# A DLRM tower on one core: the slots' products in two halves, id products for two tables only, and one engine for the slots known ahead

## What is computed

```python
e = jnp.stack([tbl_0[ids[:, 0]], ..., tbl_25[ids[:, 25]]], axis=1)
combined = jnp.concatenate((dense_features[:, None, :], e), axis=1)
interactions = jnp.einsum('bfd,bgd->bfg', combined, combined)
z = jnp.concatenate((dense_features, interactions[:, iu, ju]), axis=1)   # iu, ju: upper triangle
h = jnp.concatenate([z, r_dense_features], axis=1)
h = jnp.maximum(h @ W_top1 + b_top1, 0.0)      # 607 x 512
h = jnp.maximum(h @ W_top2 + b_top2, 0.0)      # 512 x 256
y = h @ W_top3                                 # 256 x 1
```

## Time and profile before

| | us |
|---|---|
| median of 3 runs | 106.65 (106.25 to 109.59) |
| the profiled execution | 106.54 |
| its span in the profile | 104.70 |
| outside the span | 1.84 |
| PE busy | 95.0 (91%) |
| DVE busy | 65.8 (63%) |
| ACT busy | 47.7 (46%) |
| POOL busy | 63.7 (61%) |

### The profile page before, as it was taken

The page is one execution under the profiler, slowest core; times in us unless marked ns, Lnnn a source line. Parts: engine busy times, 40 slices in busy tenths (PEclk is TensorE's granted clock), DMA queues, the critical chain, the costliest instruction groups (busy, mean ns, idle before and its releaser), DMA issues.

```text
span 104.7 us, 3425 instructions
## 1 busy us (share of the span) xinstructions
PE 95.0 (91%) x1510; PEld 81.2 (78%) x1510; DVE 65.8 (63%) x112; ACT 47.7 (46%) x83; POOL 63.7 (61%) x66
## 2 busy tenths in 40 slices
PE   5969899999999999999999589998999879994992
PEld 5846587888888888888877389986999769993990
DVE  5259999999999999999630294205741084506121
ACT  3286799998508608902300165301834039121230
POOL 2777777787787777777777377775777760000000
PEclk9999999999999999999999999999999999999999
DMA  1999999999922211211212110111111210000000
GB/s 32 205 365 422 394 386 419 416 386 409 376 96 50 53 50 47 53 44 34 56 50 66 47 49 27 50 50 50 53 50 50 50 50 25 0 0 0 0 0 1
DMA packets 3957, 12.99 MB, mean 124 GB/s; under 512 B 1447, under 2 KB 1453, under 8 KB 3310
## 3 DMA queue, kind: packets, MB, share of 16 engines
q1 hardware_dynamic: 1874, 8.95, 22.6%
q0 software_dynamic: 1920, 3.94, 13.1%
q10 hardware_dynamic: 156, 0.02, 0.1%
HBM read 12.90 MB, written 0.00 MB: 123 GB/s over the span
## 4 chain that ended last, share of the span: by engine, by line
PE 76%; DVE 12%; DMA 4%; issue 3%; ACT 2%; ACTq 1%; DVEq 0%
PE prod L361 18%; PE bank L361 16%; PE bank L404 13%; PE prod L450 11%; PE prod L477 7%; DVE inter_s L566 4%; DMA col_sb<-in_columns 4%; PE bank L370 4%; DVE mask L502 3%; DVE low L517 2%; PE bank L317 2%; PE prod L459 2%; PE bank L486 2%; PE bank L321 2%; ACT pairs_s L678 1%
## 5 line engine op out<-in xcount | busy, mean ns | idle before, releaser
L309 POOL DMA_INDIRECT emb<-in_tbl,ids_sb x60 | 63.0, 1051 | 22.0 <-issue 16.2
L502 DVE TENSOR_SCALAR mask<-ids_h,col_sb 128x1024 fp32r<-128x1024 int16 (+1 forms) x49 | 31.0, 694 | 1.9 <-ACT ids_h L639 1.6
L566 DVE STREAM_TRANSPOSE inter_s<-prod 128x288 f32<-128x288 f32 (+1 forms) x8 | 4.6, 612 | 17.9 <-PE prod L450 17.9
L450 PE MATMUL prod<-xT 128*27 128x27 f32 x1024 | 12.9, 194 | 1.9 <-issue 0.8
L361 PE MATMUL prod<-mask,high 128*128 128x512 f32 x42 | 14.0, 396 | 0.0
L361 PE MATMUL prod<-mask,low 128*128 128x512 f32 x42 | 13.8, 390 | 0.0
L450 PEld LDWEIGHTS prod<-xT 128*27 128x27 f32 x1024 | 11.1, 103 | 3.5 <-issue 3.1
L678 ACT COPY pairs_s<-inter_s 128x117 f32<-128x117 f32 x8 | 2.3, 294 | 21.5 <-DVE inter_s L566 18.9
L511 DVE TENSOR_TENSOR low<-table,high 128x1024 fp32r<-128x1024 f32 (+1 forms) x9 | 11.4, 1301 | 0.2 <-ACT high L611 0.2
L404 PE MATMUL bank<-pairs,w_sb 117*128 117x128 f32 x96 | 11.4, 275 | 0.0
L361 PE MATMUL bank<-mask,high 128*128 128x512 f32 x36 | 11.3, 395 | 0.0
(11 more groups left out here) (56 smaller groups left out, 103.9 us busy)
## 6 DMA issues: line engine op xcount, KB each, us to landing
table<-in_resident SPq DMA_DIRECT2D x3, 1024.0 KB, 8.2
w_sb<-in_weights SPq DMA_DIRECT2D x1, 1792.0 KB, 12.9
table<-in_resident SPq DMA_DIRECT2D x1, 1280.0 KB, 12.8
table<-in_resident SPq DMA_DIRECT2D x4, 256.0 KB, 4.6
emb<-in_tbl,ids_sb POOLq DMA_INDIRECT x60, 2.8
ids_h<-in_other_ids SPq DMA_DIRECT2D x1, 640.0 KB, 11.9
table<-in_resident SPq DMA_DIRECT2D x1, 640.0 KB, 8.4
known<-in_dense_t SPq DMA_DIRECT2D x1, 256.0 KB, 11.9
```

The source lines that it names most:

```text
L309: nc.gpsimd.indirect_dma_start(out=rows(t, c), out_offset=None, in_=gathered[c], in_offset=bass.IndirectOffsetOnAxis(ap=ids_sb[:, i:i + 1] ...
L450: mm = nc.tensor.matmul(prod[SLOT_PITCH * q:SLOT_PITCH * q + SLOTS, i, 0:SLOTS], x, x, start=True, stop=True)
L502: nc.vector.tensor_scalar(made(step)[:, 0:n, :], ids_h[:, 2 * b:2 * b + n, :], col_sb[:, row:row + 1], None, ALU.is_equal).then_inc(s_mask, 1)
L566: nc.vector.transpose(blocks[:, rows, 0:MATMULS], prod[:, :, rows].rearrange("p j g -> p g j")).then_inc(s_blk, 1)
```

## The change

- Only two tables' ids are spread by TensorE (`SPREAD` 2); the ids of pair 1 come by a broadcasting DMA behind table pair 1 (`pair_ids`, 256 KB), and those of the other seven tables by one behind pair 2 (`other_ids`, 896 KB). The id products contract over 2 partitions instead of 128.
- The columns are part of `ids_sb`, and their own DMA is gone.
- `WARM_UP` goes from 4 to 6, `WARM_KEEP` from 2 to 10 products of two instructions each.
- ACT makes one mask in each of pairs 1 to 4, instead of two in pair 1 and one in pair 2. DVE makes one mask between the two lower parts of a pair. `w1_sum` moves behind all masks.
- The slots' products are split in two halves, with the turns of groups 0 and 1 of the next tile between them; group 3 is turned with group 2, ahead of layer 2.
- The result of a tile is made behind the products of the next one, inside an If, and the last one after the loop. The dense part of layer 1 is made in its own tile, interleaved with the first turn of pairs and the first pairs' products.
- ACT packs all twelve known slots, and makes both halves of `h2`, packing group 3 before them. Layer 2 writes one bank, with one semaphore at its end.

```diff
@@ -41,7 +41,7 @@
...
-ON_ACT = [0, 2, 1, 0, 0, 0]
+ON_ACT = [0, 1, 1, 1, 1, 0]
...
@@ -54,10 +54,10 @@
...
-SPREAD = 6
-WARM_UP, WARM_KEEP = 4, 2
-KNOWN_ON_DVE = 6
+SPREAD = 2
+WARM_UP, WARM_KEEP = 6, 10
...
@@ -94,8 +95,8 @@
...
-        id_exact = sb("id_exact", [P, BATCH], F32R)
-        row_of = sb("row_of", [P, SPREAD, P], F32R)
+        id_exact = sb("id_exact", [SPREAD, BATCH], F32R)
+        row_of = sb("row_of", [SPREAD, SPREAD, P], F32R)
...
@@ -119,19 +119,18 @@
...
+        l2_bank = bank[2]
...
-        l2_bank = half_bank
-        id_bank = l1_bank + t_bank + [y_bank]
+        id_bank = l1_bank
...
+        s_pair_ids = sem("s_pair_ids")
...
-        s_id_zero = sem("s_id_zero")
...
-        s_row_of = sem("s_row_of")
...
@@ -255,13 +251,16 @@
...
-                    sp.dma_start(ids_h[:, SPREAD:, :], other_ids.partition_broadcast(P)).then_inc(s_other_ids, 16)
...
+                if b == 1:
+                    sp.dma_start(ids_h[:, 2:4, :], pair_ids.partition_broadcast(P)).then_inc(s_pair_ids, 16)
+                if b == 2:
+                    sp.dma_start(ids_h[:, 4:, :], other_ids.partition_broadcast(P)).then_inc(s_other_ids, 16)
...
@@ -399,6 +395,15 @@
...
+            def products(some):
+                for i in some:
+                    for q in range(QUADS):
+                        x = xT[:, i, q, 0:SLOTS]
+                        mm = nc.tensor.matmul(prod[SLOT_PITCH * q:SLOT_PITCH * q + SLOTS, i, 0:SLOTS], x, x,
+                                              start=True, stop=True)
+                return mm
...
@@ -406,22 +411,41 @@
...
-            def dense_part(samples):
-                for n in range(HID1 // P):
+            def turn_pairs(p, k):
+                pe.wait_ge(s_pick[k], p)
+                nc.tensor.transpose(pt_bank[k][0:K_PAIRS, 0:P], pairs_s[:, k, :], ident[:]).then_inc(s_ptr, 1)
+            def dense_part(samples, some):
+                for n in some:
...
+            def first_pairs(some):
+                for n in some:
+                    layer1(n, w1_pairs(0), pairs[0:K_PAIRS, 0, :], False)
...
-                    nc.tensor.matmul(half_bank[1][:, 0:P], pairs[:, 0, :], pairs[:, 0, :], start=True, stop=True)
+                    nc.tensor.matmul(half_bank[1][:, 0:P], warm, warm, start=True, stop=True)
+            def spread():
+                for r in range(SPREAD):
+                    nc.tensor.matmul(id_bank[r][:], row_of[:, r, :], id_exact[:], start=True, stop=True
+                                     ).then_inc(s_spread, 1)
+            def result(p):
+                pe.wait_ge(s_h2, p)
+                for m in range(HID2 // P):
+                    mm = nc.tensor.matmul(y_bank[0:1, 0:P], col_sb[:, W3 + m:W3 + m + 1],
+                                          h2[:, m, :], start=(m == 0), stop=(m == HID2 // P - 1))
+                mm.then_inc(s_l3, 1)
...
-            pe.wait_ge(s_row_of, 1)
-            pe.wait_ge(s_id_exact, 1)
-            for r in range(SPREAD):
-                nc.tensor.matmul(id_bank[r][:], row_of[:, r, :], id_exact[:], start=True, stop=True
-                                 ).then_inc(s_spread, 1)
+            pe.wait_ge(s_id_exact, 2)
+            spread()
...
@@ -433,34 +457,27 @@
...
-            pe.wait_ge(s_known, 2 * len(PAIRS) - 2)
-            pe.wait_ge(s_ids_h, spread_by_act(SPREAD - 1))
-            pe.wait_ge(s_w1sum, 1)
-            dense_part(slice(0, P))
...
-                pe.wait_ge(s_ready_act, p)
-                pe.wait_ge(s_ready_dve, p)
-                for i in range(MATMULS):
-                    for q in range(QUADS):
-                        x = xT[:, i, q, 0:SLOTS]
-                        mm = nc.tensor.matmul(prod[SLOT_PITCH * q:SLOT_PITCH * q + SLOTS, i, 0:SLOTS], x, x,
-                                              start=True, stop=True)
-                mm.then_inc(s_prod, 1)
+                pe.wait_ge(s_ready, 2 * p)
+                products(range(MATMULS // 2))
...
-                for k in range(K_TILES):
-                    pe.wait_ge(s_pick[k], p)
-                    if k == 0:
-                        pe.wait_ge(s_y, p)
-                    nc.tensor.transpose(pt_bank[k][0:K_PAIRS, 0:P], pairs_s[:, k, :],
-                                        ident[:]).then_inc(s_ptr, 1)
+                products(range(MATMULS // 2, MATMULS)).then_inc(s_prod, 1)
+                with nc.tensor.If(p > 1):
+                    result(p - 1)
+                samples = bass.ds((p - 1) * P, P)
+                dense_part(samples, (0, 1))
+                pe.wait_ge(s_y, p)
+                turn_pairs(p, 0)
+                dense_part(samples, (2, 3))
...
-                for n in range(HID1 // P):
-                    layer1(n, w1_pairs(0), pairs[0:K_PAIRS, 0, :], False)
+                first_pairs((0, 1))
+                turn_pairs(p, 1)
+                turn_pairs(p, 2)
+                first_pairs((2, 3))
...
@@ -468,31 +485,25 @@
...
                         mm.then_inc(s_l1, 1)
-                turn_next(p, (2,))
+                turn_next(p, (2, 3))
...
                             first = W2 + c * HID2 + m * P
-                            mm = nc.tensor.matmul(l2_bank[m][:, 0:P], w_sb[:, first:first + P], h1[:, c, :],
-                                                  start=(c == 0), stop=(c == HID1 // P - 1))
-                        if half == 1:
-                            mm.then_inc(s_l2, 1)
-                turn_next(p, (3,))
-                with nc.tensor.If(p < TILES):
-                    dense_part(bass.ds((p % TILES) * P, P))
-                for m in range(HID2 // P):
-                    pe.wait_ge((s_h2_act, s_h2_dve)[m], p)
-                    mm = nc.tensor.matmul(y_bank[0:1, 0:P], col_sb[:, W3 + m:W3 + m + 1],
-                                          h2[:, m, :], start=(m == 0), stop=(m == HID2 // P - 1))
-                mm.then_inc(s_l3, 1)
+                            mm = nc.tensor.matmul(l2_bank[:, m * P:(m + 1) * P], w_sb[:, first:first + P], h1[:, c, :],
+                                                  start=(m == 0 and c == 0), stop=(c == HID1 // P - 1),
+                                                  skip_group_check=True)
+                mm.then_inc(s_l2, 1)
+            result(TILES)
...
-                nc.vector.tensor_copy(*pack(t, g)).then_inc(s_ready_dve if g == 2 else s_pack[g], 1)
+                nc.vector.tensor_copy(*pack(t, g)).then_inc(s_ready if g == 2 else s_pack[g], 1)
...
@@ -518,18 +529,16 @@
...
-            nc.vector.memset(pairs[:, 0, :], 1.0).then_inc(s_warm, 1)
...
-            nc.vector.memset(id_exact[:].bitcast(F32), 0.0).then_inc(s_id_zero, 1)
+            nc.vector.memset(warm, 1.0).then_inc(s_warm, 1)
...
-            nc.vector.tensor_copy(row_of[:], ident[:, 0:SPREAD].unsqueeze(2).to_broadcast([P, SPREAD, P])
-                                  ).then_inc(s_row_of, 1)
+            nc.vector.tensor_copy(row_of[:], ident[0:SPREAD, 0:SPREAD].unsqueeze(2).to_broadcast([SPREAD, SPREAD, P])
+                                  ).then_inc(s_id_exact, 1)
...
-            dve.wait_ge(s_id_zero, 1)
-            nc.vector.tensor_copy(id_exact[0:SPREAD, :], id_rows[:]).then_inc(s_id_exact, 1)
+            nc.vector.tensor_copy(id_exact[:], id_rows[:]).then_inc(s_id_exact, 1)
...
-            dve.wait_ge(s_col, 16)
+            dve.wait_ge(s_ids, 16)
...
@@ -540,21 +549,22 @@
...
-                if PAIRS[b][-1] < SPREAD:
-                    dve.wait_ge(s_ids_h, spread_by_act(PAIRS[b][-1]))
+                if b == 1:
+                    dve.wait_ge(s_pair_ids, 16)
...
-                if b == RAW_PAIRS:
-                    dve.wait_ge(s_w, 16)
-                    nc.vector.tensor_tensor(w1_sum[:], w_sb[:, W1D:W1D + HID1], w_sb[:, W1D + HID1:W1D + 2 * HID1],
-                                            ALU.add).then_inc(s_w1sum, 1)
-                for r in PAIRS[b]:
-                    lower_part(r)
+                lower_part(PAIRS[b][0])
...
+                    if k == ON_ACT[b] and len(PAIRS[b]) > 1:
+                        lower_part(PAIRS[b][1])
+            dve.wait_ge(s_w, 16)
+            nc.vector.tensor_tensor(w1_sum[:], w_sb[:, W1D:W1D + HID1], w_sb[:, W1D + HID1:W1D + 2 * HID1],
+                                    ALU.add).then_inc(s_w1sum, 1)
...
-            nc.vector.tensor_copy(*pack_looked(RESIDENT - 1))
-            nc.vector.tensor_copy(*keep_looked(RESIDENT - 1)).then_inc(s_ready_dve, 1)
+            nc.vector.tensor_copy(*keep_looked(RESIDENT - 1)).then_inc(s_kept_last, 1)
+            nc.vector.tensor_copy(*pack_looked(RESIDENT - 1)).then_inc(s_ready, 1)
...
@@ -575,10 +585,6 @@
...
-                if more:
-                    if t == 0:
-                        dve.wait_ge(s_known, 2 * len(PAIRS) - 2)
-                    nc.vector.tensor_copy(*pack_known(t + 1, 0, KNOWN_ON_DVE))
...
@@ -586,16 +592,13 @@
...
-                dve.wait_ge(s_l2, t * 2 + 2)
```

(35 more changed lines are left out.)

37 lines of the change are left out of this document (18 added, 19 removed).

## The result

| | before | changed |
|---|---|---|
| median of 4 runs | 106.68 us (106.25 to 109.59) | 109.67 us (109.61 to 110.42) |
| profiled execution | 106.54 | 109.64 |
| its span | 104.7 | 107.8 |

The ratio is 1.031, 95% interval 1.0247 to 1.0373: 3.1% slower. The forecast was 108.0 us with a range from 105.5 to 109.5, so the time lies above the range, and 0.27 was all the chance that "slower by more than 2%" had. The direction of the sum was right (+1.45 us), but it was half of what came (+3.1 us in the spans).

What follows compares the result with a forecast made beforehand. Bound by TensorE's look-up, then per tile its own work plus waits for DVE and ACT. Terms -0.5, -0.2, +1.0, +0.35, +0.6, +0.2 sum to +1.45: span 106.15, plus 1.84 around it, 108.0 us; range 105.5 to 109.5.

Steps and rivals of the forecast that it cites:

- ACT's chain as the last to end: After T, the end of a tile's products: known slots, then h1, hold layer 2; next products T+9.0, +0.2 each.
- Rival (D): ACT's chain does not end last: known slots done by T+5.0, next products at T+7.5; 103.5 us, chance 0.05.
- Products 4: Last tile's products, two halves with a branch and a refill but no turns: 2.7 us against 2.35, +0.35.
- (A): Rival: no holes at all in the products, both halves 1.2 us, tile 1 also; 106.1 us, chance 0.22.
- the end: Last tile after its products: no known slots, but ACT makes both halves of h2; +0.2 us.
- layer 1 ends at T + 4.9: Layer 1's finish after the end of a tile's products; in the last tile against T+4.99 before.
- Net +0.2: Last tile's sum: layer 1 T+4.9 against 4.99, h2 0.64 against 0.36, four result instructions, not two.
- the products: Slots' products in halves of 1.4 us, turns between: +0.5 each in tiles 2 and 3, -0.2 in tile 1.
- The estimate of 97 pairs: In the products, 32 queued load-and-product pairs, used at 9.2 ns and filled at 13.7, give a lead lasting 97 pairs.
- the start: Before the look-up: fewer ids products, no wait for the columns, earlier first mask; gain 0.5 us, between 0.1 and 0.6.
- the bound of +0.7: Look-up taken as 0, with bounds 0 and +0.7 us, the latter for a mask late at pair 1.
- Rival (B): Holes in the products as now: second half loses three of 0.19, tile 1 keeps its 0.93; 109.4 us, chance 0.15.

## Why the prediction was wrong

**Right.** The bound of the look-up (no hole but the one at pair 1). ACT's chain as the last to end: h1 at T + 6.4 (forecast 6.53), layer 2 at T + 7.0 (7.2), next products at T + 9.05 (9.0), and the price per tile, +0.24 (+0.2). That the price agrees so well is partly luck, since two of its parts were off by as much in opposite directions: the copy of 1536 elements took 2.90 us, not 3.16 (the 2.07 ns an element from the earlier trace rows do not hold for one more step), and layer 2, which now waits for its input, took 2.05, not 1.79. Rival (D) is out, and the second chain that would have stood behind it shows in the run with the copy taken back: T + 7.8, near the forecast 7.5. First mask 5.60 (5.75). Products 4: 2.77 (2.7). Holes are what separates 2.35 from 3.5; (A) was half true: all second halves of tiles 2 to 4 ran at or near tile 4's rate (1.20, 1.20 and 1.27).

**Wrong: the end, +0.7 instead of +0.2.** The largest miss of a single term, and two steps of it failed. One is "layer 1 ends at T + 4.9": it ended at 102.78, T + 5.26, since I priced the group behind the wait for `pairs` at 0.112 an instruction. The first product behind a wait takes its whole length: 0.71 for the four of `first_pairs((0, 1))`, not 0.45. The other is the addition to "Net +0.2": layer 1 earlier by 0.09, `h2` later by 0.28 and two result instructions more, 0.22, make +0.4. The chain has 0.63 for both halves of `h2`, where one half took 0.36, and 0.61 for the result, where it had 0.39. Layer 2 took 1.89 in the last tile of both kernels and explains nothing. In tiles 1 to 3 most of this is hidden beneath ACT's chain; only the last tile, which has no known slots, shows it. All of this is read from the two chains of waits; no run took a part of the end alone.

**Wrong: the products, +1.5 instead of +0.8 without tile 4.** I took 1.4 us for each half, from the 126 weight loads in 1.60 us, as if a lead of the sequencer ran out. The lead is not the cause. What counts is whether POOL makes a gather meanwhile: first halves 1.74 to 1.80, second halves 1.20 in tiles 2 and 3, where the holds had stopped POOL by chance, and 1.85 in tile 1, where they had not. The estimate of 97 pairs agreed with the trace for the wrong reason. In tiles 2 and 3 the sum came out near by luck: 1.74 and 1.20 are 2.94 for the two halves, where I had 2.8; the turns took 1.02 and 1.09 instead of 0.88, and the branch 0 and 0.26 instead of 0.3. More than half of the miss is tile 1: "-0.2" was +0.2. The long hole of 0.93 did go in this trace (the largest is 0.29; in two traces of other kernels with halves one of 0.53 and one of 0.68 stay), but both halves ran beside gathers, 1.80 and 1.85.

**Wrong by a little: the start, -0.3 instead of -0.5.** 0.9 us were gained at first, more than forecast, since the 20 instructions of `WARM_KEEP` took only 2.5 us in this execution; in two variants with the same values they took 4.5 and 4.6, and the look-up products that begin at 11.56 here began at 13.37 and 13.87. That this execution gained at all was luck. The step that failed is "ACT's one mask until 15.3, and PE wants it at 16.1; I take 0 for the look-up". Table pair 1 landed at 12.0, 0.9 later than in the rows, ACT's casts ended at 14.1 and its mask at 16.2, and PE wanted it at 15.9. I had the bound of +0.7 in the text and took the other end.

**The range.** All six terms missed upward, and each by less than 0.6. The upper bounds that stand in the text (0.1 of gain at the start, 4.5 in products 2 and 3, 0.2 more in tile 1) give +3.25 and 109.8, even without the +0.7 of the look-up and before anything is missed at the end, so the range cut off at 109.5 what its own terms allowed. Rival (B), the holes as before, was the nearest in size, 109.4, but not in kind: the halves had their holes where gathers were made, and not where a lead had run out.

## What to carry to other kernels

In a loop in which one engine is nearly always busy, look at the order of the other engines' queues before moving that engine's own work: a copy that took 1.3 us longer in each of three tiles, on an engine that is idle for 60% of a tile, cost 2 us because the next layer's input stood behind it. Work moved out of the shadow of a wait (the turns of groups 0 and 1) costs its full length unless the wait is shortened by as much. And price the first instruction behind a wait with its full length, and only the rest of its group with the pace of the stream.
